# Filling eight heads' rows with one copy, splitting the first job's copies over two queues, and a new step order in a decoder block

## The chip, the cores and the metric

One core of one Trainium2 chip runs one launch of the kernel. The metric is the device time of that launch in microseconds (us). Engines: TensorE (PE, with its weight loads PEld), VectorE (DVE), ScalarE (ACT), GpSimd (POOL) and SyncE (SP, which here does nothing but issue DMAs). SPq and ACTq in the rows are DMA issues on SP's and ACT's instruction streams.

## The reference

A decoder block over x of shape (4 batches, 1024 tokens, 256):

```python
x = x + attn(layernorm(x), w_qkv, w_out)      # 16 heads of 16, chunks of 128 tokens, causal,
                                              # each chunk sees itself and the chunk before
x = x + xattn(layernorm(x), ctx, mask, Wq..)  # 77 context rows per batch, 16 heads, biases
x = x + ffn(layernorm(x), ...)                # 704 wide
# ffn: xq = fake_quant(x); gate, up = xq @ fq(w_gate).T, xq @ fq(w_up).T
#      h = fake_quant(silu(gate) * up); return h @ fq(w_down).T
# fake_quant scales by the maximum of |x| over the whole tensor, rounds to +-127
```

## The kernel before

Attention is cut into 16 **jobs** of eight heads each: S0a, S0b, S1a ... are the halves a and b of self-attention of batch 0, 1, ..., X0a ... those of cross-attention. They run in the order S0a S0b S1a S1b S2a X0a S2b X0b S3a X1a S3b X1b X2a X2b X3a X3b. A job has two **groups** g = 0, 1 of four heads, so there are 32 phases. The FFN runs after them; its quantised weights are prepared during the last four phases.

Scores are computed with Q and K split into three bf16 **parts** each, kept in `parts[128, 2, 3, tokens]` (both groups: partitions 0-63 belong to group 0, 64-127 to group 1). The matmul wants the six products of parts along the contraction, so each part is copied by DMA to rows rr, rr+6, ... below 96 of a **ring** of four slots, one per (job, group) of two jobs in flight:

```python
Q_PART = (0, 0, 0, 1, 1, 2)
K_PART = (0, 1, 2, 0, 1, 0)
```

Six copies fill Q or K of one group. They are issued by SP at line 522 (L516 for the small keys of cross-attention, from `kparts`; the first job's keys of group 0 on ACT, L959). The step of this is `("bulk", job, g, z)`, z = 0 for Q and 1 for K. A copy of a later job waits until the group two jobs before it that held the same slot has finished its last value product (L759 for S, L770 for X), and until DVE has written the last part (L1182):

```python
if AT[job] > 1:
    e.wait_ge(t_val, slot_free(job, g))    # = n_of[end_val(JOBS[AT[job] - 2], g)]
```

A phase then goes: **max** (TensorE scores by query, L679 to L688 for S and L578 for X, for the maximum; it waits for the copies through `land_q`, `land_k`; DVE reduces them, L1199 and L1203); **rows** (DVE splits the maximum into `m`, L1213 to L1219); **turnm** (TensorE transposes it, ACT casts and sends it as a row, `m3t`, L983, L985); **score** (TensorE transposed scores with that row, L578; ACT exp, L995 for S and L999 for X; POOL masks S, L1471); **val** (TensorE, L759 and L770); **evac** (ACT copies the result to `oe`, L1008, when the group before has been spread); **spread** (SP, four DMAs, L534); **gather** of the sums (ACT, L1014), **invert** (DVE), **store** and **widen** (SP, L541 and L549, the 512 KB `oc`), **scale** (DVE, L1236) and **out** (TensorE projection, L578 again).

Everything is in program order on its engine. One list of steps, made by `attention_order()`, gives that order for all engines: `PLACE` gives the stretch of a phase over which steps of a kind are spread, `LENGTH` the length of a phase, `BEHIND` how many steps later a follow-up step goes. In this list `bulk` of a job's K half follows the `split` of its projection by up to 36 steps.

At the start: x of batch 0 is loaded (L480, L481), statistics (DVE, L1149, L1151), `root` (POOL, L1461), normalisation (`xn`, DVE, L1164), transposes (TensorE, L623), the Q, K projection of S0a (L578), `split` into parts, the copies, then the first max. POOL writes four blocks of ones (L1455) behind the root; SP issues the loads of biases (L491) and of `w_out` (L500, 16 DMAs). The natural layout of w_qkv lies in ring slot 3.

Of the kernel before, what the change touches and what calls it, by code (L numbers as in the profile page):

```python
# [16 lines left out]
KX = 77  # L17
# [9 lines left out]
        for j in "S0a S0b S1a S1b S2a X0a S2b X0b S3a X1a S3b X1b X2a X2b X3a X3b".split()]  # L27
# [4 lines left out]
LENGTH = {"s": 20.85, "x": 8.51}  # L32
PLACE = {"max s0s": (0.035, 0.597), "max s1s": (-0.465, 0.137), "max s1x": (0.076, 0.64), "max x0x": (-0.066, 0.607),
# [6 lines left out]
         "shift": (-0.33, 1.48), "setup": (0.257, 0.719), "v first": (-0.955, 0.353), "qk first": (0.681, 1.752)}  # L40

BEHIND = {"scaled": 5, "turned": 1, "scaled 4": 0, "split": 1, "vmove": 0, "bulk": 36, "turnm": 2, "evac": 3,
          "spread": 0, "gather": 3, "invert": 5, "store": 7, "widen": 2, "scale": 8, "wturn": 8, "val": 2}

def follow(s):
# [12 lines left out]
    if k == "split" and s[3] == 1:  # L62
        return ("proj", BEHIND["bulk"], ("bulk", s[1], 0, s[2]))
# [60 lines left out]

def stats_steps(kind, b):
    return [("stats", kind, b, c) for c in range(NC)] + [("root", kind, b, 0, NC)]
# [39 lines left out]
def attention_order():  # L166
# [22 lines left out]
    for p in range(2 * len(JOBS)):  # L189
        n, g = divmod(p, 2)  # L190
        job, units = JOBS[n], UNITS[JOBS[n][0]]
        kind, length = job[0], LENGTH[job[0]]
        nxt = JOBS[n + 1] if n + 1 < len(JOBS) else None
        put([(-0.001, ("force", "rows"))] + over(PLACE["tail " + kind], tail))
        scores = over(PLACE["score " + kind], [("score", job, g, j) for j in range(units)])
# [5 lines left out]
        if p + 1 < 2 * len(JOBS):  # L201
            put(over(PLACE[f"max {kind}{g}{nxt[0] if g else kind}"], max_steps(p + 1)))
        last = JOBS[n - 1] if n else ("s", 0, 0)
        if g == 0:
            if nxt:
                put(over(PLACE["bulk " + kind], [("bulk", nxt, 1, z) for z in range(2)]))
                if nxt[0] == "s":
                    put(over(PLACE["v " + kind], [("v", nxt, c0) for c0 in (0, 4)]))
                else:
                    put(over(PLACE["keys " + kind], [("xkeys", nxt), ("bulk", nxt, 0, 1)]))  # L210
            if kind == "x" and job[2] == 0:
                put(over(PLACE["shift"], shift_steps(job[1])))
            if last[2] == 1 and (kind == "s" or last[0] == "x"):
                span = PLACE[f"out {last[0]}{kind}"]
                put(over(span, out_steps(*last[0:2])))
                outs_end = start + span[1] * length
            if n + 2 < len(JOBS) and JOBS[n + 2][0:2] not in normed:
                put(over(PLACE["stats " + kind], stats_steps(*JOBS[n + 2][0:2])))
                normed.add(JOBS[n + 2][0:2])
        else:  # L220
            if last == ("s", last[1], 1) and kind == "x":
                put(over(PLACE["out sx"], out_steps(*last[0:2])))
# [1341 lines left out]
```

## Time and profile before

| | us |
|---|---|
| time, median of three runs (lowest, highest) | 830.67 (829.82, 837.5) |
| profiled execution: its time, its span | 832.08, 829.9 |
| busy PE, DVE, ACT, POOL | 646.1, 521.9, 414.9, 190.0 |
| DMA moved, mean rate | 73.02 MB, 88 GB/s |

Busy PE is the time in which a matmul is under way; idle time stands in the rows as the number in brackets with what ended it. TensorE runs at a granted clock, 1.0 of full speed (2.4 GHz) or 0.5 (1.2 GHz); values between are means over a stretch.

### The profile page before, as it was taken

Reading aid. Unit: us, or ns where it says so; the run is one execution under the profiler, and the core shown is the slowest. Engines: PE = TensorE matmul, PEld = TensorE weight load, DVE = VectorE, ACT = ScalarE, POOL = GpSimd, SP = SyncE. Lnnn points to the kernel's source line nnn. Section 1 sums busy time; section 2 is a strip of 40 time slices with the busy share of each in tenths; the row PEclk is TensorE's granted clock in tenths of the full one; section 3 lists DMA queues with packets and bytes.
Section 4 is the critical chain, followed back from the end, with each engine's and each line's share of the span. In section 5 each row is a group of like instructions: output and inputs, shape, how many; then the busy total and the mean of one; then the engine's idle time right before and its main releaser. Section 6 shows DMA issues by size and latency. Waiting matters only on the chain.

```text
span 829.9 us, 33413 instructions
## 1 busy us (share of the span) xinstructions
PE 646.1 (78%) x14695; PEld 418.5 (50%) x14700; DVE 521.9 (63%) x975; ACT 414.9 (50%) x610; POOL 190.0 (23%) x231
## 2 busy tenths in 40 slices
PE   1678889899887988789798768789787685387665
PEld 1247565657654665367556544456544343133254
DVE  6277557876753559376558754375734652689896
ACT  2324656555474436445434545343442271499685
POOL 5002122323231302120204032030011000045446
PEclk9888999999997999899989999898886895599989
DMA  7435143414532243242333243331337122000023
GB/s 220 100 101 188 54 135 86 132 29 131 132 98 47 66 145 106 66 151 59 95 117 89 73 105 88 74 94 35 101 69 190 40 56 43 0 1 0 1 75 129
DMA packets 59631, 73.02 MB, mean 88 GB/s; under 512 B 25004, under 2 KB 36448, under 8 KB 59488
## 3 DMA queue, kind: packets, MB, share of 16 engines
q1 hardware_dynamic: 53391, 68.01, 29.6%
q10 hardware_dynamic: 6096, 2.88, 1.4%
q8 instruction: 117, 1.92, 1.0%
q14 instruction: 27, 0.21, 0.1%
HBM read 17.74 MB, written 4.72 MB: 27 GB/s over the span
## 4 chain that ended last, share of the span: by engine, by line
PE 18%; DVE 14%; SPq 10%; issue 6%; DMA 5%; ACT 3%; POOL 1%; POOLq 0%; ACTq 0%; DVEq 0%
PE banks L578 13%; SPq L522 4%; SPq L516 3%; DMA oc<-sums 2%; SPq L534 2%; DVE tops L1378 2%; PE banks L770 1%; DMA sums<-ls 1%; PE banks L824 1%; DVE big L1372 1%; DVE parts L1396 1%; DVE parts L1360 1%; DVE mneg L1199 1%; ACT big L999 1%; DVE parts L1397 1%
## 5 line engine op out<-in xcount | busy, mean ns | idle before, releaser
L578 PE MATMUL banks<-big 96*32 96x77 bf16 (+3 forms) x5120 | 189.5, 250 | 43.3 <-issue 14.5
L578 PEld LDWEIGHTS banks<-big 99*32 99x32 bf16 (+2 forms) x5120 | 127.6, 103 | 105.8 <-issue 63.0
L1471 POOL TENSOR_SCALAR_AFFINE_SELECT big<-big 128x512 f32<-128x512 f32 x128 | 84.2, 658 | 372.8 <-ACT big L995 370.5
L995 ACT ACTIVATE big<-banks 128x1024 f32<-128x1024 f32 (+1 forms) x128 | 122.0, 974 | 90.2 <-PE banks L578 83.7
L1199 DVE TENSOR_REDUCE mneg<-banks 128x4 f32<-128x640 f32 (+3 forms) x128 | 126.6, 1018 | 61.8 <-PE banks L688 59.9
L578 PE MATMUL banks<-xnT,weights 128*32 128x512 f32 x768 | 104.3, 664 | 0.1
L999 ACT ACTIVATE big<-banks 77x1024 f32<-77x1024 f32 x64 | 65.2, 1020 | 72.6 <-PE banks L578 72.6
L1203 DVE TENSOR_REDUCE mneg<-banks 128x8 f32<-128x616 f32 x64 | 50.0, 792 | 67.9 <-PE banks L578 67.9
L759 PE MATMUL banks<-big 128*17 128x256 f32 (+1 forms) x1152 | 80.3, 357 | 8.3 <-POOL big L1471 6.1
L679 PE MATMUL banks<-big 96*32 96x160 bf16 (+3 forms) x1792 | 78.8, 262 | 6.7 <-DVE mneg L1199 3.6
L688 PE MATMUL banks<-causal,identb 128*32 128x64 bf16 x1024 | 58.4, 199 | 4.6 <-issue 4.6
L578 PE MATMUL banks<-maskt,identb 77*32 77x512 bf16 (+1 forms) x384 | 55.3, 408 | 0.0
L824 PE MATMUL banks<-oe,weights 128*128 128x512 bf16 x187 | 46.8, 394 | 10.8 <-DVE big L1372 4.4
L679 PEld LDWEIGHTS banks<-big 96*32 96x32 bf16 x1792 | 47.6, 100 | 14.2 <-DVE mneg L1199 5.6
L578 PEld LDWEIGHTS banks<-xnT,weights 128*32 128x32 f32 x768 | 30.8, 120 | 41.2 <-issue 37.8
L770 PE MATMUL banks<-big 77*17 77x256 f32 x512 | 49.2, 397 | 2.6 <-ACT big L999 2.6
L1008 ACT COPY oe<-banks 128x512 f32<-128x512 f32 x64 | 37.3, 584 | 26.0 <-DMA oTx<-oe 11.6
L682 PE MATMUL banks<-big 96*32 96x128 bf16 x256 | 37.3, 230 | 16.1 <-DMA big<-parts 11.1
L578 PE MATMUL banks<-maskq,identb 128*32 128x308 bf16 x512 | 46.8, 340 | 0.0
L1182 DVE TENSOR_TENSOR parts<-big,parts 128x512 bf16<-128x512 f32 x48 | 34.0, 709 | 16.2 <-ACT parts L964 15.9
L688 PEld LDWEIGHTS banks<-causal,identb 128*32 128x32 bf16 x1024 | 40.4, 100 | 5.6 <-issue 5.5
L1173 DVE TENSOR_TENSOR big<-banks,parts 128x512 f32<-128x512 f32 x32 | 22.1, 690 | 31.1 <-ACT parts L952 30.7
(153 smaller groups left out, 1148.9 us busy)
## 6 DMA issues: line engine op xcount, KB each, us to landing
big<-parts SPq DMA_DIRECT2D x282, 128.0 KB, 2.5
oc<-sums SPq DMA_DIRECT2D x16, 512.0 KB, 4.5
oTs<-oe SPq DMA_DIRECT2D x64, 64.0 KB, 2.5
out_dram<-oTs SPq DMA_DIRECT2D x16, 256.0 KB, 2.1
xs<-in_x_dram SPq DMA_DIRECT2D x3, 1024.0 KB, 6.0
big<-oe SPq DMA_DIRECT2D x32, 64.0 KB, 2.5
oTx<-oe SPq DMA_DIRECT2D x32, 64.0 KB, 2.6
big<-kparts SPq DMA_DIRECT2D x96, 9.6 KB, 1.8
```

Source lines behind the costliest of these rows:

```text
L578: t = e.matmul(to[u:z], k[:, u:z], q, start=start, stop=stop, tile_position=(0, u), skip_group_check=True)
L679: e.matmul(to, q, K[0:96, hh, k0 - 128:k0 + own], start=(i == 0), stop=False, tile_position=(0, 32 * u), skip_group_check=True)
L682: e.matmul(to[:, 0:128], q, K[0:96, hh, 0:1].to_broadcast([96, 128]), start=(i == 0), stop=False, tile_position=(0, 0), skip_group_check=True)
L688: t = e.matmul(bank(p, j)[32 * u:32 * u + 32, :].rearrange("p (s n) -> p s n", s=2)[:, :, 96 + own:128 + own], identb[:, 32 * u:32 * u + 3 ...
L759: t = e.matmul(acc[:, col // 512][32 * i:32 * i + 17, col % 512:col % 512 + z - a], va[f][:, j, 4 * g + i, :], P[:, i, a:z], start=new, st ...
L770: t = e.matmul(acc[:, j // 2][32 * i:32 * i + 17, (j % 2) * 256:(j % 2) * 256 + 256], xv[r][0:KX, i, 0:17], pt[u][0:KX, i * 256:i * 256 + ...
L824: t = e.matmul(bank(p, z), wguT[:, z, i, t0 * 128:t0 * 128 + 128], xqT[blk % 2][:, i, :], start=(i == 0), stop=(i == 1))
L995: e.activation(pt[u].rearrange("p (i n) -> p i n", i=4)[:, :, 0:n], pair(p).rearrange("p j (s n) -> p (j s) n", s=2)[:, :, 0:n], ACT.Exp, ...
L999: e.activation(pt[u][0:KX, :].rearrange("p (s n) -> p s n", s=2), pair(p)[0:KX], ACT.Exp, scale=SCALE).then_inc(a_exp, 1)
L1199: e.tensor_reduce(M.rearrange("p (h c) -> p h c", h=4)[:, :, c], pair(p).rearrange("p j (s n) -> p (j s) n", s=2)[:, :, 0:160 + 32 * (c % 4)],
L1203: e.tensor_reduce(M.rearrange("p (h c) -> p c h", h=4)[:, c:c + 2, :], pair(p)[:, :, 0:4 * KX].rearrange("p j (s n) -> p j s n", s=4), AX. ...
L1471: e.affine_select(out=P[:, :, 0:128], in_=P[:, :, 0:128], compare_op=ALU.is_ge, fill=0.0, base=0, pattern=[[0, 4], [1, 128]], channel_mult ...
```

## The change

1. Both groups of a job share one ring slot of eight heads. One copy fills 16 partitions with 8 heads x 1024 tokens (256 KB, read from all 128 partitions of `parts`) where two copies of 4 heads (128 KB, read from 64 partitions) did. An S job needs 12 copies where it needed 24, an X job 6 + 6 where it needed 12 + 12. All wait for the end of group **1** of the job two before. Landing semaphores are per job, no longer per group. To allow this the columns of the Q, K weights are permuted by eight heads instead of four.
2. The first job's copies go part by part: SP issues Q's three copies of part 0 when the projection is cast, then part 1, then part 2, then K's three of part 0; ACT issues K's two of part 1 and one of part 2.
3. Ones: two blocks by DVE and two by POOL, at the very start. `mix` (POOL) comes after the first job's max. w_qkv's natural layout moves from the ring to the tile of probabilities, so the first exp waits for its last cast. Biases take 4 DMAs for 8, `w_out` 2 for 16.
4. A new order: every number of `LENGTH`, `PLACE` and `BEHIND` is new, and `FINE` gives single phases numbers of their own; `bulk` is placed by its own numbers.

```diff
-LENGTH = {"s": 20.85, "x": 8.51}
+LENGTH = {"s": 32.92, "x": 14.3}
...
+def place(name, p):
+    return FINE.get(f"{name} @{p}", PLACE[name])
...
-    if k == "split" and s[3] == 1:
-        return ("proj", BEHIND["bulk"], ("bulk", s[1], 0, s[2]))
...
-    o.run([("clear",)] + [("stats", "s", 0, c) for c in range(4)] + [("root", "s", 0, 0, 4)]
+    o.run([("first ones", 0), ("first ones", 1), ("ones", 2), ("ones", 3), ("clear",)] + [("stats", "s", 0, c) for c in range(4)] + [("root", "s", 0, 0, 4)]
...
-          + [("ones", r) for r in range(4)] + [("mix",), ("force", "norm")])
-    o.run(qk_steps(JOBS[0]) + [("force", "proj"), ("bulk", JOBS[0], 1, 0), ("bulk", JOBS[0], 1, 1)])
+          + [("force", "norm")])
+    o.run(qk_steps(JOBS[0]) + [("force", "proj"), ("bulk", JOBS[0], 0), ("bulk", JOBS[0], 1)])
...
-    o.run([("force", "proj")])
+    o.run([("force", "proj"), ("mix",)])
...
-        def slot_free(job, g):
-            return n_of[end_val(JOBS[AT[job] - 2], g)]
+        def slots_free(job):
+            return n_of[end_val(JOBS[AT[job] - 2], 1)]
...
-                for h in range(8):
-                    e.dma_start(wo[h:128:8, c, :], w_out[c * 128 + 16 * h:c * 128 + 16 * h + 16, :]).then_inc(ld_wo, 16)
+                e.dma_start(wo[:, c, :], w_out[c * 128:c * 128 + 128, :].rearrange("(h d) n -> d h n", d=HD)).then_inc(ld_wo, 16)
...
+                elif k == "bulk" and AT[s[1]] == 0:
+                    _, job, z = s
+                    for part, ready, n in ((0, a_p0, n_of["qk", job, z, 1]), (1, a_p1, n_of["split", job, z, 1]),
+                                           (2, d_p2, n_of["split", job, z, 1]))[:1 if z else 3]:
+                        e.wait_ge(ready, n)
...
                     else:
                         e.wait_ge(d_p2, n_of["split", job, z, 1])
                         for rr in range(6):
-                            e.dma_start((qs, ks)[z][r][rr:96:6, :, :],
-                                        parts[64 * g:64 * g + 64, z, (Q_PART, K_PART)[z][rr], :]
-                                        ).then_inc((land_q, land_k)[z][r], 16)
+                            e.dma_start(ring[rr:96:6, r // 2, z].rearrange("p g h t -> p (g h) t"), parts[:, z, (Q_PART, K_PART)[z][rr], :]
+                                        ).then_inc((land_q, land_k)[z][r // 2], 16)
...
                     if c == 0:
-                        e.wait_ge(land_q[r], landed(job, g))
-                        e.wait_ge(land_k[r], landed(job, g))
+                        e.wait_ge(land_q[r // 2], landed(job))
+                        e.wait_ge(land_k[r // 2], landed(job))
...
+                    if n_of[s] == 1:
+                        e.wait_ge(a_wqkv, 3)
...
+                elif k == "first ones":
+                    e.memset(ones[s[1]], pair_of_ones).then_inc(d_ones, 1)
```

**Place 1: POOL and DVE at the start.** POOL of before, from the zeroed pieces of `big` (L1442) on; the 32x2048 memsets are the ones:

```order
L1442 MEMSET big 128x64 x2
L1461 TENSOR_TENSOR rstd<-ve,halves 128x4 x2
L1455 MEMSET big 32x2048 x4
L1450 COPY oc<-xnT 128x4x8x16
L1471 AFFINE_SELECT big<-big 128x4x128 x3
```

POOL of the change at the same place:

```order
L1505 MEMSET big 128x64 x2
L1516 MEMSET big 32x2048 x2
L1522 TENSOR_TENSOR rstd<-ve,halves 128x4 x2
L1513 COPY oc<-xnT 128x4x8x16
L1532 AFFINE_SELECT big<-big 128x4x128 x4
```

The memsets stand ahead of the root. DVE of the change begins so:

```order
L1180 CAST identb<-ident 128x128
L1191 MEMSET big 32x2048 x2
L1193 MEMSET banks 128x1024
L1213 BN_STATS st<-xs 128x6
```

DVE had no 32x2048 memset before; it now has two ahead of the first statistics.

**Place 2: SP around the copies of X3a**, the last but one job. `big<-parts` are copies of Q, `big<-kparts` of keys, `big<-oe` and `oTx<-oe` spreads, `sums<-ls` and `oc<-sums` store and widen. Before:

```order
L516 DMA big<-kparts 16x4x77 x6
L522 DMA big<-parts 16x4x1024 x12
L516 DMA big<-kparts 16x4x77 x6
L534 DMA big<-oe 16x1024 x4
L541 DMA sums<-ls 128x64
L549 DMA oc<-sums 128x1x1024
L534 DMA oTx<-oe 16x1024 x4
```

The change; copies of 16x8x1024 and 16x8x77 are of both groups:

```order
L585 DMA big<-parts 16x8x1024 x6
L596 DMA big<-oe 16x1024 x4
L603 DMA sums<-ls 128x64
L579 DMA big<-kparts 16x8x77 x6
L611 DMA oc<-sums 128x1x1024
L596 DMA oTx<-oe 16x1024 x4
```

Ahead of the first spread stand 6 copies where 24 stood, and X3a's keys are copied behind it and its store.

**Place 3: TensorE ahead of the first max of S2b**, behind the last value product of S2a (32x77 with `maskq` is a max of X0a, 32x256 with 13x256 and `maskt` a score of X0a, `weights,xnT` half of a v step of S2b, `identb,m` the transposes of the maximum; L682, now L744, begins the max of S2b). Before:

```order
L578 MATMUL banks<-big 32x77 x16
L578 MATMUL banks<-maskq,identb 32x308 x4
L578 MATMUL banks<-big 32x77 x16
L578 MATMUL banks<-maskq,identb 32x308 x4
L578 MATMUL banks<-weights,xnT 32x128 x32
L682 MATMUL banks<-big 32x128
```

The change:

```order
L640 MATMUL banks<-maskt,identb 32x512 x2
L640 MATMUL banks<-maskt,identb 13x512
L640 MATMUL banks<-big 32x256 x2
L640 MATMUL banks<-big 13x256
L640 MATMUL banks<-big 32x256 x2
L640 MATMUL banks<-big 13x256
L640 MATMUL banks<-maskt,identb 32x512 x2
L640 MATMUL banks<-maskt,identb 13x512
L640 MATMUL banks<-identb,m 32x128 x3
L640 MATMUL banks<-weights,xnT 32x128 x32
L744 MATMUL banks<-big 32x128
```

More of X0a's scores, the transposes and the second half of v now stand ahead of S2b's max.

## Rows read from the trace of the kernel before

**Rows 1.** Profile page: engines' busy time (share, instructions), granted TensorE clock per slice.
```profile
PE 646.1 (78%) x14695; PEld 418.5 (50%) x14700; DVE 521.9 (63%) x975; ACT 414.9 (50%) x610; POOL 190.0 (23%) x231
PEclk9888999999997999899989999898886895599989
```

**Rows 2.** Page: the chain that ended last, by engine and by line.
```profile
PE 18%; DVE 14%; SPq 10%; issue 6%; DMA 5%; ACT 3%; POOL 1%; POOLq 0%; ACTq 0%; DVEq 0%
PE banks L578 13%; SPq L522 4%; SPq L516 3%; DMA oc<-sums 2%; SPq L534 2%; DVE tops L1378 2%; PE banks L770 1%; DMA sums<-ls 1%; PE banks L824 1%; DVE big L1372 1%; DVE parts L1396 1%; DVE parts L1360 1%; DVE mneg L1199 1%; ACT big L999 1%; DVE parts L1397 1%
```

**Rows 3.** The waits: engine, line, waited for: us, times, longest.
```profile
PE banks L623 <- DVE xn L1164: 20.3, 11, 12.4
PE banks L682 <- DMA big<-parts: 11.1, 2, 8.8
...
PE banks L578 <- ACT big L999: 9.0, 6, 3.3
...
PE banks L578 <- DMA big<-m3t: 7.2, 4, 2.5
PE banks L578 <- DMA big<-kparts: 5.8, 4, 1.9
```

**Rows 4.** Timeline of the start: start us, duration, engine, line, tiles [idle before <- releaser].
```profile
11.93 1.38 DVE L1164 TENSOR_SCALAR xn<-xs,mv,rstd 128x256 f32<-128x256 f32 x4
13.40 7.48 POOL L1455 MEMSET big<- 32x2048 f32 x4
14.48 6.55 DVE L1164 TENSOR_SCALAR xn<-xs,mv,rstd 128x256 f32<-128x256 f32 x4 [1.18 <-PE banks L623]
...
33.98 5.76 ACTq L959 DMA_DIRECT2D big<-parts  x6
43.46 0.27 PE L682 MATMUL banks<-big 96*32 96x128 bf16 x1 [8.78 <-DMA big<-parts]
```

**Rows 5.** Source views of lines 522, 516 and 534 (DMA issues).
```profile
L522 SPq DMA_DIRECT2D big<-parts x282: 545/598/2074, 33.2 to 631.7; - x141
DMA to landing us min/median/max: 2.2/2.5/3.5
L516 SPq DMA_DIRECT2D big<-kparts x96: 545/594/1782, 246.0 to 638.9; - x96
  ACT oe L1008: 26.0, 7
```

**Rows 6.** Windows: stretch, length, busy us of PE, PEld, DVE, ACT, POOL, clock, DMA share, GB/s.
```profile
3.00:6.00 3.00, 0.00 (x0) 0.00 (x0) 0.00 (x0) 0.00 (x0) 0.00 (x0) 1.00 1.00 339
33.00:44.00 11.00, 2.22 (x88) 1.98 (x80) 0.87 (x2) 1.30 (x3) 0.00 (x0) 0.68 0.82 205
628.00:640.00 12.00, 9.40 (x211) 6.71 (x205) 2.47 (x4) 1.08 (x2) 0.00 (x0) 0.50 0.84 219
```

**Rows 7.** Timeline around the ends of S0a and S2a.
```profile
107.06 0.81 PE L759 MATMUL banks<-big 128*17 128x256 f32 x13
122.23 1.76 DVE L1199 TENSOR_REDUCE mneg<-banks 128x4 f32<-128x640 f32 x2
...
286.13 1.11 PE L759 MATMUL banks<-big 128*17 128x256 f32 x16
294.94 0.22 PE L682 MATMUL banks<-big 96*32 96x128 bf16 x1 [2.33 <-DMA big<-parts]
```

**Rows 8.** Timeline: waits behind a late SP queue.
```profile
465.80 0.24 PE L578 MATMUL banks<-identb,m 128*32 128x128 bf16 x3 [3.17 <-DVE m L1219]
587.01 8.89 SPq L522 DMA_DIRECT2D big<-parts  x12
606.31 0.59 ACT L1008 COPY oe<-banks 128x512 f32<-128x512 f32 x1 [5.57 <-DMA big<-oe]
607.87 0.61 PE L578 MATMUL banks<-big 99*32 99x256 bf16 x6 [3.31 <-ACT big L999]
647.91 1.08 PE L578 MATMUL banks<-weights,big 128*32 128x256 f32 x8 [4.42 <-DVE oTx L1236]
```

More of the change, by code:

```diff
@@ L190, in attention_order, with at @@
         n, g = divmod(p, 2)
+        def at(name):
+            return place(name, p)
         job, units = JOBS[n], UNITS[JOBS[n][0]]
@@ L193, in attention_order @@
         nxt = JOBS[n + 1] if n + 1 < len(JOBS) else None
-        put([(-0.001, ("force", "rows"))] + over(PLACE["tail " + kind], tail))
-        scores = over(PLACE["score " + kind], [("score", job, g, j) for j in range(units)])
+        put([(-0.001, ("force", "rows"))] + over(at("tail " + kind), tail))
+        scores = over(at("score " + kind), [("score", job, g, j) for j in range(units)])
         for j in range(units):
@@ L201, in attention_order @@
         if p + 1 < 2 * len(JOBS):
-            put(over(PLACE[f"max {kind}{g}{nxt[0] if g else kind}"], max_steps(p + 1)))
+            put(over(at(f"max {kind}{g}{nxt[0] if g else kind}"), max_steps(p + 1)))
         last = JOBS[n - 1] if n else ("s", 0, 0)
@@ L205, in attention_order @@
             if nxt:
-                put(over(PLACE["bulk " + kind], [("bulk", nxt, 1, z) for z in range(2)]))
+                put(over(at("bulk " + kind), [("bulk", nxt, z) for z in range(2)]))
                 if nxt[0] == "s":
-                    put(over(PLACE["v " + kind], [("v", nxt, c0) for c0 in (0, 4)]))
+                    put(over(at("v " + kind), [("v", nxt, c0) for c0 in (0, 4)]))
                 else:
-                    put(over(PLACE["keys " + kind], [("xkeys", nxt), ("bulk", nxt, 0, 1)]))
+                    put(over(at("keys " + kind), [("xkeys", nxt)]))
             if kind == "x" and job[2] == 0:
-                put(over(PLACE["shift"], shift_steps(job[1])))
+                put(over(at("shift"), shift_steps(job[1])))
             if last[2] == 1 and (kind == "s" or last[0] == "x"):
-                span = PLACE[f"out {last[0]}{kind}"]
+                span = at(f"out {last[0]}{kind}")
                 put(over(span, out_steps(*last[0:2])))
@@ L229, in attention_order @@
         if p in setup_at:
-            put(over(PLACE["setup"], [step for part in setup_at[p] for step in part]))
+            put(over(at("setup"), [step for part in setup_at[p] for step in part]))
         if p in xload_at:
@@ L346, in build @@
         maskn = oTx[:, 0:NC * KX].bitcast(I32).rearrange("p (c k) -> p c k", c=NC)
-        wqkvn = ring[:, 3, 1].rearrange("p h t -> p (h t)").bitcast(F32)[:, 0:1536].rearrange("p (c n) -> p c n", c=2)
-        ones = [ring[96:128, r, 1].rearrange("p h t -> p (h t)").bitcast(F32) for r in range(4)]
+        wqkvn = big[:, 16384:17920].rearrange("p (c n) -> p c n", c=2)
+        ones = [ks[r][96:128].rearrange("p h t -> p (h t)").bitcast(F32) for r in range(4)]
         pair_of_ones = float(np.array([0x3F803F80], dtype=np.uint32).view(np.float32)[0])
@@ L711, in run_tensor @@
                         if AT[job] < 2:
[L712 removed]
+                            e.wait_ge(*((d_ones, r + 1) if r < 2 else (p_ones, r - 1)))
                     if job[0] == "s":
@@ L947, in run_scalar @@
                     if before and blk == 0:
-                        for g in range(2):
-                            e.wait_ge((land_q, land_k)[z][slot(before, g)], landed(before, g))
+                        e.wait_ge((land_q, land_k)[z][AT[before] % 2], landed(before))
                     P = parts[:, z, 0, blk * 512:blk * 512 + 512]
@@ L955, in run_scalar @@
                 elif s == first_keys:
-                    job, g = s[1:3]
-                    e.wait_ge(d_p2, n_of["split", job, 1, 1])
-                    for rr in range(6):
-                        e.dma_start(ks[slot(job, g)][rr:96:6, :, :], parts[64 * g:64 * g + 64, 1, K_PART[rr], :]
-                                    ).then_inc(land_k[slot(job, g)], 16)
+                    for rr in (1, 4, 2):
+                        e.wait_ge(*((a_p1, d_p2)[K_PART[rr] - 1], n_of["split", JOBS[0], 1, 1]))
+                        e.dma_start(ring[rr:96:6, 0, 1].rearrange("p g h t -> p (g h) t"), parts[:, 1, K_PART[rr], :]
+                                    ).then_inc(land_k[0], 16)
                 elif k == "split":
@@ L1314, in run_vector @@
                     if n_of[s] == 1:
-                        for g in range(2):
-                            e.wait_ge(land_k[slot(("s", NB - 1, 1), g)], landed(("s", NB - 1, 1), g))
+                        e.wait_ge(land_k[AT["s", NB - 1, 1] % 2], landed(("s", NB - 1, 1)))
                     e.tensor_scalar(w_i8[0:w, at:at + w_width[z]], w_nat[z][0:w, t0, :], winv[0:w, col:col + 1], None,
@@ L1357, in run_vector @@
                             e.wait_ge(a_wb, 14)
-                            for r in range(4):
+                            for r in range(2):
                                 e.wait_ge(land_q[r], 96 * 8)
```

87 lines of the change are left out of this document (43 added, 44 removed), and 64 rows, old and new, of tables (FINE, PLACE).

## The prediction

> **What bounds the kernel now.** I read the page first: TensorE is busy for 646.1 us of the span and its clock is near full in most slices [rows 1]. So no single engine is full, and what can be won is TensorE's idle time, where it ends the run. The chain that ended last is the second view: next to PE 18% it gives SPq 10% and DMA 5%, by line L522 4%, L516 3% and L534 2% [rows 2]. That is the issuing of copies, which computes nothing. The third view, the waits, says what TensorE itself lost: 20.3 us for `xn` (12.4 of it one wait, for the first tile), 11.1 us in two waits for `big<-parts`, 5.8 for `kparts`, 7.2 for the row `m3t`, 9.0 for ACT's exp [rows 3]. Then the timeline, for the reasons. At the start POOL's memsets of ones run from 13.40 to 20.88, and DVE's four `xn` operations beside them take 6.55 us, where the four before took 1.38 [rows 4]. The first max starts at 43.46 after 8.78 us of waiting for its copies; ACT's six issues end at 39.74 [rows 4]. Later, SP issues 282 and 96 copies at a median of 598 and 594 ns each, 226 us of a queue in program order [rows 5]. What stands behind them is late: 12 copies take SP from 587.01 to 595.90, ACT can empty its banks only at 606.31, 5.57 us after it was ready, because the spread ahead of it had not landed, its exp is late, and TensorE loses 3.31 us [rows 8].
>
> **The change part by part.**
>
> *Ones and start.* Two memsets go to DVE, where the 7.48 us for four give 1.87 each, 3.7 us. DVE has nothing to do until x lands: with its banks memset (under 1 us) it is done ahead of the first statistics, which need the loads of 3 to 6 us [rows 4, 6]. POOL's two end before the root. So four `xn` cost 1.38 instead of 6.55: **-5.2 us**. The projection follows each transpose and moves by the same. Were the memsets late, two would push the statistics by up to 3.7 us, the rest of the gain. `mix` goes behind the first max, where POOL waits for ACT; bias and `w_out` loads drop 18 issues from SP, whose start of copies at 33.2 [rows 5] was set by the split, not by them: nothing, but the part-by-part copies need SP free earlier, and this makes it so.
>
> *First copies.* The last split was at 33.95 (before ACT's first issue at 33.98) and moves to 28.8. Half of the bytes (part 0 of Q, then of K) can go before it. But the first max now waits for both groups: 12 copies of 256 KB, 3.15 MB, where it waited for 12 of 128 KB with six more between. Bounds: started at about 24 and running at the 205 GB/s of the stretch 33 to 44, 15.3 us and 2.5 to land: 41.8, which against 38.3 (43.46 less the 5.2) is +3.5 us; at the 339 of the loads 9.3 us, so that the last split decides, with six copies behind it, 4 us of issue and 2.5 to land: 35.3, -3.0 [rows 4 to 6]. In the stretch the DMA share was 0.82, and 205/0.82 is 250 GB/s, 12.6 us: 39.1. Issue on ACT takes 0.96 us each (5.76/6) and three are left of six. As the copies of group 1 are then already there too, where before 12 more stood behind, I take **-3**, the near end.
> The row shows 205 GB/s for copies whose source is 64 partitions and 339 for a load that writes 128 [rows 6]. The Trainium skill, "SBUF — State Buffer", section "Door 1: The DMA port swizzle (why [64,N] ≈ [32,N])", says that a transfer over 64 partitions reaches 8 of 16 ports and one over 128 reaches all. By that, the larger copies would run up to twice as fast on their source side; on the destination side (16 partitions) it promises nothing, and the sum does not use it. Against the two-queue part speaks "DMA: Bandwidth & Descriptors", section "Issuing engines are not separate DMA queues": a second engine only saves issue time, not transfer time. By that, the copies on ACT would save at most their own three issues, about 2 us, and the -3 would be nearer -1.
>
> *Half the copies.* SP issues 189 fewer, 189 x 0.598 = 113 us less of its queue. That is worth only what waited for it: the two kinds of waits of TensorE for copies after the start, 11.1 - 8.8 = 2.3 and 5.8, together **-8.1**; and waits of others behind the queue: 9.0 for exp, 4.42 (647.91, behind spread and scale), 3.17 (465.80, where DVE was held by `oc<-sums`), 2.5 for `m3t`, 19.1 in all [rows 3, 8]. Ahead of the first spread of that place stand 6 copies and not 24. Not all will go, since stores and widens keep their latency: I take half, **-9.6** (bounds 0 and -19.1).
>
> *The later gate.* Copies for group 0 waited for the end of group 0 two jobs before, 20 to 40 us ahead of their use; now all wait for group 1. What is between? For S1a it was 107.87 to 122.23, 14.3 us; for S2b 287.24 to 294.94, 7.7 us [rows 7]. I added TensorE's instructions between the two points in the new order, at their durations in the trace, times 1.18 (what such stretches really took against that sum). Free time until the first max: S1a 12.6, S2b 9.2, S3a 9.9, S3b 10.9, X2a 9.3, X3a 9.3, X3b 8.0, the other jobs 11.7 to 18. Needed: 12 copies at 339 GB/s 9.3 + 2.5 = 11.8, at 250 15.1; I take 13 for an S job. An X job needs 6 of 256 KB and 6 small ones: 6.3 us of bytes at 250 GB/s, or 12 issues at 0.6 less what overlaps, and landing: 10.3. New stalls: S1a 0.4, S2b 3.8, S3a 3.1, S3b 2.1, X2a 1.0, X3a 1.0, X3b 2.3: **+14**. Bounds: 4 at 339 GB/s; at 205 an S job needs 17.8 and an X job 13.3, and summed over all jobs this is +53. In the new order more work stands here than before in S2b (scores, transposes, half of v), which is why it is not more.
>
> *Other moves.* w_qkv in the tile of probabilities makes the first exp wait for a cast of before the first projection, long done: nothing. The five loads of FFN weights now stand between X3b's Q and K copies; they already did so once, and were hidden. The order's other distances (row to score, max to row) go both ways by 1 to 7 us of work; I take 0, bounds ±8.
>
> Sum from the profiled 832.1: -5.2 -3 -8.1 -9.6 +14 = 820.2. The profiled run is 1.4 above the median: **819 us**.
>
> **The rivals.**
> - *B, relief given back.* The start is won, the queue's relief is all eaten by the later gate: 830.7 - 8.2 + (between 0 and 8) = about **825**. For it: the gate price (+14) is of the size of the relief (-17.7), and a wait for ACT's exp may be ACT's own. Within 1%.
> - *D, better than the sum.* All late waits go (-9.6 more) and the 128-partition source lets copies run at 339 GB/s, so that the gate costs 4 instead of 14: 819 - 9.6 - 10, = 799, with 4 lost elsewhere **803**. For it: 339 at 3 to 6 us; against: that load had no 16-partition destination.
> - *C, slower: the gate of both groups decides.* If twelve copies of 256 KB run at 205 GB/s, each S job waits 5 to 9 us and each X job 2 to 5: +53 instead of +14, 819 + 39 = **858**. In 628 to 640 the share was 0.84 at 219 GB/s and the clock at half, 0.50 [rows 6]; a stall that lets the clock fall adds to it. It decides from about 15.5 us per S job on: that is 20 more over some nine jobs with no slack left, and 819 + 20 is 1% above the median.
> - *E, the new order does nothing but move waits* and the copies' size changes no wait: the gain is only the start, 822; this lies between A and B and is counted there.
>
> **How the numbers follow.** This kernel's measurement tells about 1% (8.3 us) from no change. A, 819 and around it (812 to 826): 0.54. B 0.22, D 0.14, C 0.10. The range leaves out C and the low end of D: 803 to 830. Faster by over 1% (under 822.4) are D and most of A, 0.66; within 1% B and the rest, 0.24; slower 0.10.
>
> **What would show it.** Right: the second four `xn` in about 1.4 us; first max at 35 to 38; waits of TensorE for `kparts` gone; SP never 12 copies behind a spread; waits for `big<-parts` at S2b, S3a, S3b of 2 to 4 us each with the copies starting at the end of group 1. Wrong: a rate near 205 GB/s in 12-copy pieces with waits over 6 us (C); no waits for copies at all (D); waits for `oe`, exp or `oc` as before (B); or a start in which `xn` still takes 6 us because something else of POOL runs beside it.

## The result, and the profile after

The changed kernel takes 854.16 us (median of four runs, 852.51 to 857.25) against 830.25 for before: ratio 1.034, 95% interval 1.029 to 1.039. It is slower by about 24 us. Ratios, here and below, compare only executions in the faster of two states in which the chip runs a program, while a median is of all executions, so a ratio can differ from the quotient of two medians. The prediction said 819, range 803 to 830, and gave 858, the rival in which the later gate decides, a chance of 0.10. The profiled execution has a span of 855.3 us, 25.4 more than before.

The page's engines and clock, then the chain that ended last. TensorE is busy for 7 us less than before and idle for 32 more [rows 1]; in the chain `big<-parts` now stands as time of the DMA itself, not only of its issue [rows 2]. The shares of the two chains can't be set against each other: the chain before adds up to 57% of its span, this one to 98%.

```profile
PE 639.2 (75%) x14700; PEld 426.6 (50%) x14700; DVE 523.6 (61%) x977; ACT 414.4 (48%) x610; POOL 185.1 (22%) x229
PEclk9788989989999989997999798988968795799979
...
PE 38%; DVE 19%; DMA 13%; issue 11%; SPq 8%; ACT 7%; POOL 1%; ACTq 1%; POOLq 0%; DVEq 0%
PE banks L640 25%; DMA big<-parts 7%; SPq L585 6%; DVE mneg L1263 4%; PE banks L821 3%; ACT big L1057 3%; DMA ls<-oe 2%; PE banks L741 2%; PE banks L832 2%; DVE tops L1441 1%; PE banks L685 1%; SPq L579 1%; PE banks L886 1%; DMA big<-m3t 1%; DMA big<-kparts 1%
```

The waits of TensorE (total, times, longest), against [rows 3]:

```profile
PE banks L744 <- DMA big<-parts: 43.5, 7, 11.0
PE banks L685 <- DVE xn L1228: 16.1, 5, 12.6
PE banks L640 <- DMA big<-kparts: 15.3, 3, 12.2
PE banks L640 <- DMA big<-m3t: 1.7, 3, 0.9
```

Copies: 11.1 us in two waits have become 43.5 in seven, keys 5.8 have become 15.3. The waits that a late queue made are shorter, `m3t` from 7.2 to 1.7. Where the copies' time goes shows in the source view of the changed line 585 (against [rows 5]), in SP's timeline around S2b, in the row of S2b's first max, and in two windows, each from the end of group 1 two jobs before to the landing:

```profile
L585 SPq DMA_DIRECT2D big<-parts x132: 557/607/1527, 53.3 to 650.6; - x132
DMA to landing us min/median/max: 3.2/6.6/10.2
```

```profile
299.04 8.80 SPq L585 DMA_DIRECT2D big<-parts  x12
...
316.89 0.27 PE L744 MATMUL banks<-big 96*32 96x128 bf16 x1 [8.67 <-DMA big<-parts]
```

```profile
299.10:316.80 17.70, 7.66 (x275) 6.20 (x263) 3.83 (x7) 3.90 (x6) 4.60 (x4) 0.90 0.93 198
109.80:127.00 17.20, 11.59 (x359) 8.52 (x347) 6.63 (x10) 6.72 (x11) 2.59 (x5) 0.86 0.95 204
```

SP starts the twelve copies at 299.04, at the end of S2a's group 1, and is through in 8.80 us. But a copy lands a median of 6.6 us after its issue, where it was 2.5, and at most 10.2: the queue no longer bounds, the transfers do, at 198 to 204 GB/s with the DMA engines 93 to 95% busy. The last one lands nearly 18 us after the gate. TensorE had 9 us of work and waits 8.67. (The windows' GB/s are of all that moves: 3.5 MB at S2b, 3.15 of them the twelve copies.)

The start did what was forecast for `xn`, and not for the copies. Before, then the change; L1182, now L1246, writes the last part:

```profile
21.71 9.48 PE L578 MATMUL banks<-xnT,weights 128*32 128x512 f32 x64
...
32.49 1.46 DVE L1182 TENSOR_TENSOR parts<-big,parts 128x512 bf16<-128x512 f32 x2
```

```profile
14.64 1.38 DVE L1228 TENSOR_SCALAR xn<-xs,mv,rstd 128x256 f32<-128x256 f32 x4 [1.17 <-PE banks L685]
...
16.75 7.07 PE L640 MATMUL banks<-xnT,weights 128*32 128x512 f32 x64
...
25.12 1.46 DVE L1246 TENSOR_TENSOR parts<-big,parts 128x512 bf16<-128x512 f32 x2
...
38.35 0.27 PE L744 MATMUL banks<-big 96*32 96x128 bf16 x1 [11.03 <-DMA big<-parts]
```

The second four `xn` take 1.38 us (6.55 before), and the first max starts at 38.35. That is 5.1 us earlier than before [rows 4]. The last part, though, was ready 7.4 us earlier (26.58 for 33.95): the projection starts 5.0 us earlier, which is `xn`, and takes 7.07 us for 9.48. From the last part to the first max the change needs 11.8 us where the kernel before needed 9.5, so the new first copies cost 2.3 us and gave nothing. Why the projection was shorter is open: the granted clock is 1.00 in both, and in the next run, with the same `xn`, it took 9.15.

### The profile page after: what moved, and what is told of

It reads as the page before. It is cut to its first block, busy times and chain, and to the rows that moved or that the text cites. A ratio compares the mean times of both kernels' runs of the same rounds, so it can differ in the third digit from the quotient of the medians.

```text
span 855.3 us, 33194 instructions
## 1 busy us (share of the span) xinstructions
PE 639.2 (75%) x14700; PEld 426.6 (50%) x14700; DVE 523.6 (61%) x977; ACT 414.4 (48%) x610; POOL 185.1 (22%) x229
## 4 chain that ended last, share of the span: by engine, by line
PE 38%; DVE 19%; DMA 13%; issue 11%; SPq 8%; ACT 7%; POOL 1%; ACTq 1%; POOLq 0%; DVEq 0%
PE banks L640 25%; DMA big<-parts 7%; SPq L585 6%; DVE mneg L1263 4%; PE banks L821 3%; ACT big L1057 3%; DMA ls<-oe 2%; PE banks L741 2%; PE banks L832 2%; DVE tops L1441 1%; PE banks L685 1%; SPq L579 1%; PE banks L886 1%; DMA big<-m3t 1%; DMA big<-kparts 1%
## 5 line engine op out<-in xcount | busy, mean ns | idle before, releaser
L640 PE MATMUL banks<-big 96*32 96x77 bf16 (+3 forms) x5120 | 186.9, 248 | 43.7 <-DMA big<-kparts 15.3
L640 PE MATMUL banks<-xnT,weights 128*32 128x512 f32 x768 | 94.2, 603 | 0.7 <-DVE big L1237 0.4
L741 PE MATMUL banks<-big 96*32 96x160 bf16 (+3 forms) x1792 | 84.8, 279 | 4.0 <-DVE mneg L1263 2.0
L744 PE MATMUL banks<-big 96*32 96x128 bf16 x256 | 40.9, 245 | 51.3 <-DMA big<-parts 43.5
L744 PEld LDWEIGHTS banks<-big 96*32 96x32 bf16 x256 | 27.6, 110 | 60.2 <-issue 54.0
L640 PE MATMUL banks<-maskt,identb 77*32 77x512 bf16 (+1 forms) x384 | 57.1, 419 | 0.0
L741 PEld LDWEIGHTS banks<-big 96*32 96x32 bf16 x1792 | 48.2, 105 | 14.9 <-issue 5.7
L832 PE MATMUL banks<-big 77*17 77x256 f32 x512 | 55.0, 416 | 0.7 <-ACT big L1061 0.7
L886 PE MATMUL banks<-oe,weights 128*128 128x512 bf16 x192 | 47.1, 392 | 10.2 <-DVE big L1435 4.4
L1246 DVE TENSOR_TENSOR parts<-big,parts 128x512 bf16<-128x512 f32 x48 | 33.8, 705 | 22.2 <-ACT parts L1024 21.7
L640 PE MATMUL banks<-weights,xnT 128*32 128x128 f32 x1024 | 34.9, 282 | 13.4 <-issue 12.9
```

What stands on the lines that cost most here:

```text
L640: t = e.matmul(to[u:z], k[:, u:z], q, start=start, stop=stop, tile_position=(0, u), skip_group_check=True)
L741: e.matmul(to, q, K[0:96, hh, k0 - 128:k0 + own], start=(i == 0), stop=False, tile_position=(0, 32 * u), skip_group_check=True)
L744: e.matmul(to[:, 0:128], q, K[0:96, hh, 0:1].to_broadcast([96, 128]), start=(i == 0), stop=False, tile_position=(0, 0), skip_group_check=True)
L832: t = e.matmul(acc[:, j // 2][32 * i:32 * i + 17, (j % 2) * 256:(j % 2) * 256 + 256], xv[r][0:KX, i, 0:17], pt[u][0:KX, i * 256:i * 256 + ...
L886: t = e.matmul(bank(p, z), wguT[:, z, i, t0 * 128:t0 * 128 + 128], xqT[blk % 2][:, i, :], start=(i == 0), stop=(i == 1))
```

## Experiments

Two theories stood at the beginning. **Gate** (theory 1 below): copies for both groups wait for group 1 two jobs before and land too late. **Order**: the new step order costs by itself. Ratios are to the kernel before, run on the same chip.

**The start alone.** The kernel before with part 3 of the change (ones, `mix`, w_qkv's place), the loads of biases and `w_out` as before:

```diff
+    o.run([("first ones", 0), ("first ones", 1), ("ones", 2), ("ones", 3), ("clear",)] + ...
-          + [("ones", r) for r in range(4)] + [("mix",), ("force", "norm")])
+          + [("force", "norm")])
```

> The kernel before with the start alone changed: two blocks of ones by VectorE and two by GpSimd at the very start, mix after the first max, w_qkv's natural layout in the tile of probabilities. Copies, gates and order numbers are those of before. Theory 1 (the loss lies in the later gate, the start is a gain of its own): the second four xn take 1.4 us, first max at 43.46 - 5.2 = 38.3, total 830.25 - 5 = 825. Rival (the start's gain is taken back by the queue or the clock behind it): first max at 38.3, total 830.

Measured: 823.32 us, ratio 0.995 (0.991 to 1.000). The four `xn` take 1.38 us and the first max of the profiled run starts at 39.18 (43.46 before). The start is worth about 4 us, a little under the 5 of theory 1; the interval only just leaves out no change.

**Eight-head copies with the old numbers.**

```diff
-LENGTH = {"s": 32.92, "x": 14.3}      # and PLACE, BEHIND, FINE of the change
+LENGTH = {"s": 20.85, "x": 8.51}      # and PLACE, BEHIND of before, FINE = {}
```

> The changed kernel with the order numbers of before (LENGTH, PLACE, BEHIND; no FINE); the eight-head copies and their later gate stay. Theory 1 (gate): a piece of 12 copies lands 17.3 us after the end of group 1; TensorE's work between was 5.8 us for S2b, S3a, S3b, so each waits about 10 us, and X3b too; waits for copies sum to 50 to 60 us and the time is about 860. Rival (the new order is at fault): back to 825 to 835.

Measured: 871.67 us, ratio 1.053 (1.039 to 1.068). The waits and S2b's first max:

```profile
PE banks L696 <- DMA big<-parts: 48.5, 5, 12.8
PE banks L592 <- DMA big<-kparts: 12.5, 3, 11.1
...
315.98 0.26 PE L696 MATMUL banks<-big 96*32 96x128 bf16 x1 [12.27 <-DMA big<-parts]
```

The gate theory holds: the old order leaves less work behind the gate, and the wait at S2b is 12.3 us. With these copies the new order is no culprit; with it the ratio is 1.034 and not 1.053, though the two intervals touch.

**Half the bytes.** The second half of each row of Q and K is left as it was, so the result is on other numbers:

```diff
+                            H = S if AT[job] < 2 else S // 2
-  e.dma_start(ring[rr:96:6, ...], parts[:, z, (Q_PART, K_PART)[z][rr], :])
+  e.dma_start(ring[rr:96:6, ...][:, :, 0:H], parts[:, z, (Q_PART, K_PART)[z][rr], 0:H])
```

> The changed kernel; every copy of big from parts of the third job on carries 512 of 1024 tokens (the rest of the row keeps old data, so part of the computation is on other numbers). As many copies, as many rows, half the bytes. If bytes set the 17.3 us from gate to landing: it falls to 9 to 11 us, the waits for copies nearly vanish, time about 812. If the number of rows or copies sets it: 17 us and 854 as before.

Measured: one execution, 807.18 us, span 805.4. At S2b:

```profile
282.12 9.61 SPq L586 DMA_DIRECT2D big<-parts  x12
...
293.69 0.27 PE L746 MATMUL banks<-big 96*32 96x128 bf16 x1 [3.50 <-DMA big<-parts]
```

From 282.12 to 293.69 are 11.6 us, where the full bytes took 17.9. Issue alone is 9.6 of these, so it is now the queue that bounds. With as many copies and rows, 47 us of the kernel's time hang on the bytes. TensorE's waits for copies hold only half of that: they fell by 24.6 us, from 43.5 + 15.3 to 20.1 + 14.1. Its busy time fell by 14.3 (639.2 to 624.9, at a mean granted clock of 0.92 for 0.89) and its waits put down to issue by 12.8. So a late copy costs more than the wait in which it shows.

**Copies of four heads in the new order.** The kernel of the first run with `LENGTH`, `PLACE`, `BEHIND` and `FINE` of the change; group 0's copies stand 12 steps behind the split and wait for group 0, as before:

```diff
-BEHIND = {..., "bulk": 36, ...}
+BEHIND = {"bulk": 12, ...}            # the other numbers are those of the change
```

> The new order and the new start with the copies of before: 128 KB for one group, group 0 waiting for the end of group 0 and group 1 for that of group 1, the first group's copies 12 steps behind the split. Theory 1 (gate): waits for big<-parts shrink to the start's and a few us, kparts to under 6; 854 - 42 less 10 to 15 us of late-queue waits that come back: 820 to 827. Rival (the new order costs by itself): 845 to 855.

Measured: 852.53 us, ratio 1.028 (1.019 to 1.037). The copies' waits went as the gate theory says, and the time did not:

```profile
PE banks L636 <- DVE oTx L1298: 22.2, 2, 12.4
PE banks L636 <- ACT big L1055: 22.0, 10, 7.9
...
PE banks L740 <- DMA big<-parts: 10.0, 1, 10.0
```

```profile
280.81 19.96 SPq L580 DMA_DIRECT2D big<-parts  x24
300.86 2.93 SPq L592 DMA_DIRECT2D oTs<-oe  x4
...
305.60 0.58 ACT L1068 COPY oe<-banks 128x512 f32<-128x512 f32 x1 [6.37 <-DMA oTs<-oe]
307.15 0.62 PE L737 MATMUL banks<-big 96*32 96x256 bf16 x8 [4.42 <-ACT big L1059]
```

24 copies hold SP for 19.96 us, the spread comes behind them, ACT empties its banks 6.37 us late, exp is late, TensorE loses 4.42. In sum, the waits for ACT's exp are 43.8 us where the kernel before had 19.1, and those for `oTx` 22.2 where it had 14.3. The new order costs 3% with the old copies. My expectation of 820 to 827 was wrong: I had counted 10 to 15 us for late-queue waits, and the time is about 30 us more than without them. By its ratio this kernel, with neither the late gate nor the large copies, is hardly faster than the changed one (1.028 and 1.034, the intervals overlap). Its distance of 12 steps, for 36 before, was my choice and wasn't varied.

**Rows side by side.** The destination rows of a part next to each other, for Q and keys:

```diff
-ring[rr:96:6, r // 2, z]
+ring[16 * rr:16 * rr + 16, r // 2, z]
```

> The changed kernel with the 16 rows of a part next to each other (16 rr to 16 rr + 15) in place of every sixth, for queries and keys alike. Bytes, copies and order are the same. If the spread of the 16 destination rows over the partitions sets the rate (12 copies in 17.3 us, 180 to 210 GB/s): the time from gate to landing grows, to 25 us and more if only a part of the ports is reached, and the kernel is slower by 30 us or more. If the rate is that of the engines or of the source: 17.3 us and 854, as before.

Measured: one execution, 989.72 us. The window from gate to landing at S2b:

```profile
360.50:390.60 30.10, 9.87 (x306) 8.52 (x297) 3.55 (x7) 3.90 (x6) 4.59 (x4) 0.73 0.98 116
```

The same twelve copies take 30 us at 116 GB/s, with the DMA engines 98% busy. So the choice of destination rows moves the rate by a factor of 1.7, and the busy share of the DMA does not show it. The Trainium skill, "SBUF — State Buffer", section "Door 1: The DMA port swizzle (why [64,N] ≈ [32,N])", gives 104 GB/s as measured for a transfer over partitions 0 to 15, which reach 4 of 16 ports. The trace agrees: 16 rows side by side are 4 such ports, and 116 GB/s, of which the twelve copies alone are 105, is near it.

**A later first max.** A pass over the steps moves the first max of nine jobs behind more of TensorE's work, 15.2 us by mean durations for S and 10 for X, and X3b's keys go ahead of the FFN weights:

```diff
+def attention_order():
+    return later_max(plain_order(), WANT, GAP)
+WANT = {"s": 15.2, "x": 10.0}         # second run: 12.5 and 9.5
```

> The changed kernel in which the first max of nine jobs is moved behind more of TensorE's other work, so that 15.2 us of work (by the mean durations; some 17.5 in the trace) for S jobs and 10 for X jobs lie between the end of group 1 two jobs before and the first max, and X3b's keys are copied ahead of the FFN weights. Theory 1 (gate): the 35 us of waits for big<-parts behind the start and 12 of kparts nearly vanish, time 815 to 830. Rival (TensorE has no work that fills it; rows and scores are late instead): waits for m, m3t or exp grow by as much and the time is over 845.

> As the run before with 12.5 us of work for S jobs and 9.5 for X: 2 to 3 us of waiting for copies stay at S2b, S3a and S3b, but the rows of S2b and S3b are less late. Theory 1: between 815 and 835, near the run before. Rival: over 845.

Measured: 874.34 us, ratio 1.069 (1.057 to 1.081), and 862.14 us, ratio 1.053 (1.037 to 1.069). In the first, only the start's wait for `big<-parts` is left, and others have grown past the gain:

```profile
PE banks L698 <- DVE m L1341: 22.7, 17, 4.1
PE banks L698 <- DMA big<-m3t: 21.2, 8, 3.9
PE banks L698 <- DVE oTx L1358: 20.5, 2, 10.8
...
PE banks L698 <- DVE oTs L1358: 12.1, 3, 10.3
PE banks L802 <- DMA big<-parts: 10.2, 1, 10.2
```

`m3t` 21.2 us (1.7 in the changed kernel), `oTx` 20.5 (11.3), `oTs` 12.1 (1.1): the rows of the maximum, the scores behind them and with these the whole pipeline of a phase are late. The rival was right. At this place a late copy costs less than a max that is put off to make room for it.

**X3b's keys first.**

```diff
-        "bulk x @28": (0.026, 0.658),
+        "bulk x @28": (0.026, 0.058),
```

> The changed kernel with one number changed, so that SP issues X3b's copies of keys ahead of the five loads of FFN weights (2.2 MB) and not behind. Theory: the 12.2 us wait for kparts at X3b falls to 2 to 4, the time to 845 to 848. Rival (the copies of Q are what is late, or the spread behind the loads becomes late): the wait moves and the time stays at 854.

Measured: one execution, 846.11 us. SP's queue in the changed kernel and TensorE's wait, then the wait with the edit:

```profile
647.33 3.90 SPq L585 DMA_DIRECT2D big<-parts  x6
...
655.51 4.18 SPq L579 DMA_DIRECT2D big<-kparts  x6
666.42 0.45 PE L640 MATMUL banks<-big 96*32 96x77 bf16 x16 [12.23 <-DMA big<-kparts]
```

```profile
648.59 0.45 PE L640 MATMUL banks<-big 96*32 96x77 bf16 x16 [4.43 <-DMA big<-kparts]
```

The five loads stood between Q and the keys; 12.23 us became 4.43, and the time is 8 us lower. On that chip the kernel before was faster too (823.38), so by ratio it is 1.028 for 1.034, 5 to 6 us.

**Other destination rows.** On top of the last edit:

```diff
-ring[rr:96:6, ...]
+rows(ring[...], rr)      # ap[32 + rr:96:4] if rr < 4 else ap[rr - 4:32:2]
```

> The changed kernel with X3b's keys ahead of the weights (the edit that gave 846) and with other destination rows for each part: copies 0 to 3 fill every fourth row from 32 to 95 (32 + rr, 36 + rr, ...), copies 4 and 5 every second row below 32. Bytes, copies, order and gates stay. The run with rows side by side took 30 us from gate to last landing where every sixth row took 17, so the choice of destination rows sets the rate. Theory (destination): a job of 12 copies lands in 12 to 13 us and the first max starts at 34 to 35; the waits for big<-parts fall from 39 to 15 us and the time to 820 to 827. Rival (side by side was slow for a reason of its own, and every sixth row is already as fast as the engines go): 17 us, 846. The Trainium skill, SBUF - State Buffer, section Door 1, says that a partition's bits 4 to 2 and 6 choose one of 16 ports: by it every sixth row reaches 13 ports with two rows on three of them, the new rows of four copies of six 16 ports with one each, and side by side 4 ports.

Measured: 835.97 us, ratio 1.013 (1.004 to 1.022). The twelve copies of a job did not land in 12 to 13 us:

```profile
285.50:302.60 17.10, 7.61 (x279) 6.21 (x264) 3.72 (x7) 3.94 (x6) 4.62 (x4) 0.80 0.85 205
302.75 0.27 PE L748 MATMUL banks<-big 96*32 96x128 bf16 x1 [9.19 <-DMA big<-parts]
```

17.1 us at 205 GB/s against 17.7 at 198. But 205 is a mean of two rates. The same stretch in four windows, and below it the middle of the stretch at S2b in the changed kernel:

```profile
287.50:290.50 3.00, 3.00 (x125) 2.90 (x122) 1.76 (x4) 1.05 (x2) 2.70 (x3) 1.00 0.94 307
291.50:293.50 2.00, 2.00 (x64) 1.68 (x61) 0.00 (x0) 0.99 (x2) 0.00 (x0) 1.00 1.06 204
293.50:296.50 3.00, 0.06 (x3) 0.00 (x0) 0.00 (x0) 0.58 (x1) 0.00 (x0) 0.85 1.08 337
296.50:300.50 4.00, 0.00 (x0) 0.00 (x0) 0.00 (x0) 0.00 (x0) 0.00 (x0) 0.50 1.00 148
```

```profile
301.00:314.00 13.00, 6.13 (x201) 5.02 (x195) 2.42 (x6) 3.37 (x5) 2.78 (x3) 0.98 1.07 225
```

Fast, slow, fast, slow is the order of the copies: 0 to 3 of Q (every fourth row from 32), 4 and 5 of Q (every second row below 32), then the same for the keys. At S3a such windows read 309, 222, 348 and 201. So the rows do set the rate: four copies of six gained a third and more over the 225 of every sixth row, and the other two lost most of it again. From the first issue to the first max, S1a, S2a, S2b, S3a and S3b take 16.3 to 17.3 us here and 17.4 to 17.9 in the changed kernel. That a window belongs to certain copies is read from their order; no run has one kind of rows alone. The Trainium skill, "SBUF — State Buffer", section "Door 1: The DMA port swizzle (why [64,N] ≈ [32,N])", agrees in order: by its port formula copies 0 to 3 reach 16 ports and were fastest, every sixth row reaches 13 (14 for two of the six copies), copies 4 and 5 reach 8 and were slowest. My estimate from it, two thirds of the 17 us, was too good, since it had copies 4 and 5 no slower than before.

The time, by ratio, is 1.013 for 1.028 with the keys' edit alone, which had one execution. TensorE's waits for `big<-parts` are no shorter (43.2 us for 39.0); those put down to issue are 12.4 for 26.3, which I can't explain by the rows.

> The kernel before with the start of the change (as in the first run, 0.995 of before) and the same new destination rows for its copies of four heads. If the issue of 24 copies on SP (0.6 us each and more) bounds a job's copies there, little changes: 0.99 to 0.995. If the destination rows bound them too: the waits of late spreads shrink as well, 0.98.

Measured for the same rows in the kernel with the old copies and the new start: 819.0 us, ratio 0.991 (0.988 to 0.995), against 0.995 with every sixth row. The intervals overlap, so the rows' own part there isn't settled.

**The late gate alone.** Copies of four heads, old order, new start, and group 0 waits for group 1:

```diff
-            return n_of[end_val(JOBS[AT[job] - 2], g)]
+            return n_of[end_val(JOBS[AT[job] - 2], 1)]
```

> The kernel of the first run (start changed, copies of four heads, order of before; 0.995 of before) with one edit: the copies of group 0, too, wait for the end of group 1 two jobs before. Sizes, count and order of the copies stay. Theory (the gate is the loss, not the size of the copies): group 0's 12 copies land some 12 us after the gate and wait where TensorE has 6 to 9 us of work (S2b, S3a, S3b, X3b), and the spreads behind them are later: 1.02 to 1.04 of before. Rival (the gate was slack with these copies and only the 256 KB copies, which take 17 us to land, make the loss): 0.995 to 1.00.

Measured: 895.79 us, ratio 1.080 (1.074 to 1.086). This run isolates the gate, with the copies and the order of before: one number in one wait takes 0.995 to 1.080. The waits, and SP's queue at S1a in this run and in the start-only run:

```profile
PE banks L680 <- DMA big<-parts: 25.5, 4, 10.6
...
PE banks L576 <- ACT big L999: 19.2, 6, 7.0
PE banks L757 <- POOL big L1471: 19.1, 10, 6.0
```

```profile
103.38 20.23 SPq L520 DMA_DIRECT2D big<-parts  x24
123.66 3.12 SPq L532 DMA_DIRECT2D oTs<-oe  x4
```

```profile
93.73 19.52 SPq L520 DMA_DIRECT2D big<-parts  x24
113.30 3.53 SPq L532 DMA_DIRECT2D oTs<-oe  x4
```

TensorE's waits for copies grew by only 10.9 us against the start-only run (12.8 + 7.0 to 25.5 + 5.2), while the span grew by 63.0. The rest is what is queued behind. The 24 copies held SP in one piece before, too; what is new is that SP stands at the gate first and begins them 9.65 us later, and the spread behind them goes out 10.4 us later. ACT's banks, exp and POOL's masks wait for it: TensorE's waits for the exp of L999 grew from 5.0 to 19.2 us, those for POOL from 6.0 to 19.1. I had left that out of the 1.02 to 1.04. Read with the second run, the eight-head copies are themselves a help once the gate is late: 1.080 becomes 1.053, though with them came the first job's part-by-part copies and the fewer loads.

**Part by part for one group.** The best of the runs that compute everything:

```diff
+                elif k == "bulk" and s[1:3] == (JOBS[0], 0) and s != first_keys:
+                    for z, part, ready, n in ((0, 0, a_p0, ...), (0, 1, a_p1, ...), (0, 2, d_p2, ...), (1, 0, a_p0, ...)):
+                        e.wait_ge(ready, n)      # then the copies of this part, group 0 only
```

> The kernel of run e12 (0.991 of before) with the first job's copies part by part, but those of group 0 alone first: SP issues six of Q and three of K part 0 as each part is ready, ACT the other three, then SP those of group 1; w_out loads in 2 DMAs for 16, so that SP is free at 23 us. Theory: half the bytes of the changed kernel stand ahead of the first max, which starts at 33 to 34 us for 38.3; 0.986 of before. Rival (TensorE's next wait takes it): 0.991.

Measured: 816.8 us (median of four, 807.6 to 822.69), ratio 0.978 (0.970 to 0.986), faster than both kernels.

```profile
35.00 0.26 PE L690 MATMUL banks<-big 96*32 96x128 bf16 x1 [5.33 <-DMA big<-parts]
```

The first max starts at 35.00, 3.4 us ahead of the changed kernel's, and 3.7 ahead of the 38.71 of the run it is built on: part by part pays when the first max doesn't wait for the other group's bytes as well. The ratio fell by more than that, 0.991 to 0.978, some 11 us; the rest isn't explained.

## Why the prediction was wrong

**The start.** Right for `xn`: -5.2 forecast, -5.0 to the start of the projection. The term of the first copies was -3 and came to about +2.3: the last part was ready at 26.58, earlier than the 28.8 of the sum, and the first max still came only at 38.35. That it is 5.1 us earlier, the size of `xn` alone, is chance, since 2.4 us of a shorter projection made up for the copies. I took "the near end" of 35.3 to 41.8 with the reason that group 1's copies would be there too; that doesn't shorten anything. 12 copies of 256 KB from 21.07 on need until about 38 at the rate of the run. The run with group 0 alone first (35.00) shows what the idea is worth.

**Waits for copies of before (-8.1) and half of the late-queue waits (-9.6).** TensorE's waits for copies behind the start went from 2.3 + 5.8 = 8.1 to (43.5 - 11.0) + 15.3 = 47.8 us. With these and -5.1 for the start, the 25.4 us of the span leave -5.1 + 39.7 + x = 25.4, x = -9.2, for everything else. That it is near -9.6 is in part chance, since 6.9 us less of busy time and 4.5 more of waits put down to issue are in it. The waits behind a late queue themselves (exp 19.1 to 13.9, `m3t` 7.2 to 1.7, `oTx` 14.3 to 11.3, `m` 14.0 to 16.6) fell by 11.1 together, so the size of this term was right.

**The gate (+14).** This is the step that failed. The mechanism was right: copies start at the end of group 1, and S2b, S3a, S3b and X3b wait. The size was 47.8 in place of 14. Two numbers made most of it. First the rate: I put 13 us for an S job's twelve copies, between 250 GB/s (the 205 of the stretch divided by its DMA share 0.82) and the 339 of a load. The runs show 17.2 to 17.9 us, 198 to 204 GB/s at a share of 0.93 to 0.95; the price of rival C, 17.8 us at 205 GB/s, was the right one. Dividing by the share was a mistake: fully busy, in the middle of the stretch, these copies ran at 225 GB/s and not at 250, and side by side at 116 with a share of 0.98, so the share tells how long the engines were held and not what they could move. Taking 339 into the mean made it worse. The free times I had worked out for the three large waits were good: with 17.4 us in place of 13 they give 8.2 at S2b, 7.5 at S3a and 6.5 at S3b, and the trace has 8.67, 8.06 and 6.26. For other jobs they were not: S1a waited 1.30 us where 17.4 would give 4.8, S2a waited 5.74 and S1b 2.48 where the sum has nothing. (The 14.3 us for S1a before end at a row of DVE, 122.23; TensorE's first max there started at 121.48.) Second, X3b: I wrote that the FFN loads between its Q and keys "were hidden". 2.2 MB on busy engines are ahead of the keys, and the wait was 12.2 us for the 2.3 of my sum; moving the keys took 7.8 us off it.

**"Of 113 us less of SP's queue only what waited for it counts"** held. But the sentence was one-sided: shorter issue also means that the transfers, not the issue, become the bound, and they ran at the rate which the stretch of 33 to 44 had shown already.

**The rivals.** C came true, at 854 for 858, with its mechanism, and I gave it 0.10. That the number is so near is in part luck: its prices of 4 us for X3a and 5.3 for X3b met 0.23 and 12.23. The rates that spoke for it, 205 and 219 GB/s, were the only two rows of such copies; the 339 was a load from HBM to other rows, and it should have been the far bound and not half of the mean. B (relief given back) was right in kind and too small. D fell.

**The two rules of the Trainium skill that the prediction names.** That of "SBUF — State Buffer", section "Door 1: The DMA port swizzle (why [64,N] ≈ [32,N])", bore nothing on the source side: windows with copies from 64 partitions read 205 and 219 GB/s, those with copies from 128 read 198 and 204. The 16 destination rows may have hidden a gain; no run changes the source alone. That of "DMA: Bandwidth & Descriptors", section "Issuing engines are not separate DMA queues", agrees with the trace: with three of the twelve first copies on ACT, all were issued at 28.97, and the first max still came 9.4 us later, with the DMA engines 86% busy.

**What is shown and what not.** Shown: the late gate costs 8.5% with the copies and order of before (0.995 to 1.080), most of it through what is queued behind the copies; bytes, not issue, bound the twelve eight-head copies; the 16 destination rows set their rate. The ratio is 1.053 with eight-head copies and the old order, 1.034 with the new order on top. Not shown: what the gate alone costs in the changed kernel, since with the new order the old copies and gates gave 1.028; whether those 3% come from the queue alone; and why waits put down to issue change between runs.

## What to carry to other kernels

When two transfers are joined into one, ask first what each waited for: the joined one waits for the later of the two, and what is queued behind it waits as well. Before, S1a's copies began 22.6 us ahead of its first max (98.85 and 121.48); slack of that kind can be what keeps the pipeline running. Price a transfer by the rate at which the same kind of copy ran when it was saturated, and do not scale that rate up by an idle share. Which rows a copy fills belongs to its kind. And when a queue gets shorter, look for what stood in its shadow: here the transfers themselves.

## What the runs showed of the hardware

The rate of an SBUF to SBUF copy to 16 partitions hangs on which 16 they are. With the DMA engines fully busy it was 225 GB/s for every sixth row (198 to 204 over the whole of a job's copies), 122 for 16 side by side (116 over the whole), 307 to 348 for every fourth row from 32 to 95, and 148 to 222 for every second row below 32. The busy share, 0.93 to 1.09 in all of these (it can read a little over 1), does not tell them apart.

VectorE's `xn` beside GpSimd's memsets took 6.55 us for four, and 1.38 without them, a factor of 4.7. It went at the pace of the memsets, 1.87 us each: TensorE's transposes behind the four `xn` of before start at 15.41, 17.30, 19.20 and 21.09.

```profile
15.41 0.69 PE L623 MATMUL banks<-ident,xn 128*128 128x128 f32 x2 [1.05 <-DVE xn L1164]
17.30 0.69 PE L623 MATMUL banks<-ident,xn 128*128 128x128 f32 x2 [1.21 <-DVE xn L1164]
...
21.09 0.69 PE L623 MATMUL banks<-ident,xn 128*128 128x128 f32 x2 [1.20 <-DVE xn L1164]
```
